# 68 of 204 expert tiles placed in the second half of the pass before them

## The chip, the cores and the metric

The kernel runs on one core of one Trainium2 chip. The metric is the device time of one execution in microseconds (us). The core has five engines, each with a program of its own that it runs strictly in order: PE (matrix multiply), DVE (vector), ACT (scalar functions), POOL (here it writes the descriptors of indirect transfers) and SP (here it issues plain transfers). They meet only through semaphores: an engine that waits for one holds back all that stands behind the wait in its program.

## What is computed

A graph layer over 12500 nodes of 256 numbers: an attention over edges (`gnn`), a linear attention over all nodes (`mix`), and then a mixture of experts on the sum. Only the last part is touched:

```python
x = x + gnn(xn) + mix(xn)                     # rows of 256, two norms inside
# then, with xn = layernorm(x) * gamma + beta:
logits = einsum('bsd,de->bse', xn, Wr) + br
top_vals, top_idx = top_k(logits, 2)          # 2 of 8 experts for each row
w = softmax(top_vals)
for e in range(8):
    h = gelu(xn @ W1[e] + b1[e])              # 256 -> 512
    y += (h @ W2[e] + b2[e]) * w_full[..., e]
x = x + y
```

## The kernel before

All stages before the last two stay as they are. The node rows stand in 98 tiles of 128 rows, in 14 chunks of 7 (CHUNK, CHUNKS).

**The pass** is `finish` (line 1479). It goes over the 14 chunks in a software pipeline; a step is one turn n of DVE's loop (line 1977). In step n DVE does `divide(n)` (L1831 scales the chunk, L1834 adds the residual row `xn` once it is loaded, then statistics), `gat_scale(n)`, `join(n-1)` (L1853 to L1862, with the other rows `hh` and `x_row`, then statistics), `choose(n-2)` (the two experts of every row, L1886 on), `ffn_scale(n-1)`, `take_slots(n-2)` and `tag(n-2)` (where each row goes in its expert's region, ending at L1946). ACT does the square roots, the affine parts (`scale_tiles`, L1721 and L1722; `make_rows`, L1742 and L1746) and the softmax's exponential; PE transposes the finished rows for the router (`turn_rows`, L1772 and L1777) and counts ranks (`rank`). POOL scatters the rows of a chunk into the experts' regions in DRAM, 14 indirect transfers a chunk (L1700). SP stores each joined chunk to `out` and loads the chunk two ahead: store, `xn`, `hh`, `x_row`, 0.9 MB each, in that order. Once in the pass it loads the weights of all eight experts, 8.4 MB, at L1656 and L1657, ahead of the loads of the last chunk. Two calls of `fold_bias` on PE (L1796) fold a vector into the first bias. Behind the last chunk DVE lists for each of 204 tiles its expert, its first row and how many adds must be done before its own (L1993 to L2031).

**The expert tiles** are `run_experts` (line 2040), in a block of their own that starts when all engines have left the pass. A tile is 128 rows of one expert. SP loads its rows (ring of 8), PE transposes them (`turn_rows`, L2139), multiplies by W1 (`up`, L2149) and W2 (`down`, L2158), ACT does gelu between (L2174), DVE copies the transposes (L2188), copies W1 to a fixed place (L2193), makes the weights and adds the bias (L2198 to L2215), and POOL adds the rows to `out` by an indirect transfer with addition (L2123). Every engine handles tile `it` together with earlier ones: PE does transposes of `it`, down of `it-3`, up of `it-1`; DVE the copies of `it`, the gate of `it-1`, the bias of `it-2` and the last addition of `it-3`. Rings of two buffers tie them: transposes of `it` wait for the copy of `it-2`, up of `it-1` for the copy of `it-1`. An add waits until all adds of earlier experts are done, since two of them may meet in a row.

## Time and profile before

| | us |
|---|---|
| median of 3 runs | 3553.38 (3551.12 to 3561.58) |
| the profiled execution | 3556.23 |
| its span, first to last instruction | 3554.6 |
| start of step 9, 10, 13 of the pass | 2528.72, 2560.27, 2652.57 |
| last routing work on DVE | 2728 |
| first up of an expert tile | 2771.67 |

All times of the trace count from the first instruction of the profiled execution. A timeline row gives the start, the duration, the engine, the source line, the operation with what it writes and reads, and in brackets how long the engine had been idle and what ended that. A row of stretches gives the length, then for each engine busy time and number of instructions (PE, PE's weight loads, DVE, ACT, POOL), then the granted clock of PE as a share of 2.4 GHz, the mean share of busy time of the 16 DMA engines and GB/s.

### The profile page before, as it was taken

The page shows a single profiled execution, that of the slowest core. Times are in us where ns is not written, and L with a number is a line of the kernel's source. Part 1 is how long each engine was busy: PE and PEld are TensorE (multiplying, and loading weights), DVE is VectorE, ACT ScalarE, POOL GpSimd, SP SyncE. Part 2 cuts the span into 40 slices and gives each one's busy share as a digit, 9 for nine tenths or more (in the row PEclk, how much of TensorE's full clock was granted, in tenths as well). Part 3 has the DMA queues.
Part 4 walks back from the last instruction along what each step waited for, and adds up shares of the span by engine and source line. Part 5 has one row for each costly group of instructions (what it writes and reads, how often), then busy time and mean ns, then how long its engine had stood idle before and what let it go on. Part 6 is the DMA issues. An engine that isn't in the chain of part 4 may idle for free. (4 is left out here: it accounts for less than half of the span.)

```text
span 3554.6 us, 70140 instructions
## 1 busy us (share of the span) xinstructions
PE 2799.0 (79%) x17326; PEld 2288.6 (64%) x17327; DVE 2343.5 (66%) x6416; ACT 1273.4 (36%) x4243; POOL 2154.7 (61%) x2117
## 2 busy tenths in 40 slices
PE   6758888889989978888888888433344899999997
PEld 4635666666666756666666666323334799999997
DVE  6656666666666667777777777888877455555554
ACT  5723333333333323333333333355542233333332
POOL 3167777777777776666666666246666344444443
PEclk9979999999999989999999999755555899999999
DMA  7645656666666666666666666445582344444443
GB/s 248 240 130 156 159 158 160 161 159 162 163 163 164 162 157 185 180 177 182 178 175 174 171 174 171 130 158 177 183 281 103 74 70 71 71 71 69 72 71 52
DMA packets 384652, 529.69 MB, mean 149 GB/s; under 512 B 64276, under 2 KB 323559, under 8 KB 384218
## 3 DMA queue, kind: packets, MB, share of 16 engines
q0 software_dynamic: 114496, 265.49, 31.9%
q1 hardware_dynamic: 185112, 183.84, 17.5%
q10 hardware_dynamic: 84770, 77.19, 6.8%
q8 instruction: 112, 1.84, 0.2%
q14 instruction: 162, 1.33, 0.1%
HBM read 394.80 MB, written 132.72 MB: 148 GB/s over the span
## 5 line engine op out<-in xcount | busy, mean ns | idle before, releaser
L1133 POOL DMA_INDIRECT rows<-node_rows,index x1552 | 1476.2, 951 | 566.3 <-issue 447.5
L1411 PE MATMUL ps_sum<-msg,hot 128*128 128x260 f32 x3904 | 1015.0, 405 | 18.4 <-DVE big L1230 2.6
L1411 PEld LDWEIGHTS ps_sum<-msg,hot 128*128 128x128 f32 x3904 | 727.5, 196 | 133.1 <-issue 7.8
L1213 DVE TENSOR_TENSOR msg<-rows,ps_w 128x1024 f32<-128x1024 f32 x488 | 595.9, 1221 | 38.0 <-ACT ps_w L1305 22.4
L2123 POOL DMA_INDIRECT out_dram<-big x204 | 353.1, 1731 | 437.2 <-DVE big L2215 388.0
L2174 ACT ACTIVATE x_actT<-x_ps_hT,b1T 128x128 f32<-128x128 f32 x816 | 232.8, 368 | 523.8 <-PE x_ps_hT L2149 523.8
L1189 DVE TENSOR_SCALAR hotT<-targets,pair_node_id 128x512 bf16 x488 | 187.0, 383 | 344.3 <-SPq L1095 340.5
L2149 PEld LDWEIGHTS x_ps_hT<-x_rowsT,x_w_now 128*128 128x128 f32 x3264 | 399.0, 193 | 11.5 <-DVE x_w_now L2193 1.1
L1391 PE MATMUL ps_hot<-ident_h,hotT 128*128 128x128 bf16 x1952 | 194.9, 223 | 268.2 <-DVE hotT L1189 266.0
L2149 PE MATMUL x_ps_hT<-x_rowsT,x_w_now 128*128 128x128 f32 x3264 | 400.1, 276 | 0.7 <-DVE x_w_now L2193 0.7
L1700 POOL DMA_INDIRECT expert_in<-f_rows,f_slot x196 | 259.4, 1323 | 223.7 <-ACT f_rows L1742 166.7
L2158 PE MATMUL x_ps_out<-big,x_actT 128*128 x1632 | 385.9, 379 | 0.0
L1391 PEld LDWEIGHTS ps_hot<-ident_h,hotT 128*128 128x128 bf16 x1952 | 128.9, 99 | 363.2 <-DVE hotT L1189 351.9
L1298 ACT ACTIVATE e<-e 128x16 f32<-128x16 f32 x488 | 106.3, 218 | 660.7 <-DVE e L1207 657.3
L2158 PEld LDWEIGHTS x_ps_out<-big,x_actT 128*128 128x128 f32 x1632 | 294.2, 190 | 31.7
L1293 ACT ACTIVATE hot<-ps_hot 128x512 f32<-128x512 bf16 x488 | 286.6, 587 | 41.0 <-PE ps_hot L1391 38.9
L2188 DVE COPY x_rowsT<-x_ps_t 128x256 f32<-128x256 f32 x204 | 86.6, 425 | 253.7 <-PE x_ps_t L2139 253.7
L1230 DVE TENSOR_TENSOR big<-big,ps_sum 128x260 f32 x488 | 202.4, 415 | 8.0 <-issue 4.8
L1759 PE MATMUL f_ps_rank<-f_taken,f_earlier 128*128 128x56 f32 x28 | 9.4, 440 | 250.0 <-DVE f_taken L1908 250.0
L1423 PE MATMUL ps_kv<-wq,area 128*128 128x512 f32 x392 | 193.6, 617 | 9.5 <-DVE area L1239 8.8
L1279 DVE TENSOR_TENSOR area<-ps_kv,area 128x256 f32<-128x256 f32 x98 | 41.6, 425 | 210.7 <-PE ps_kv L1468 210.7
L2215 DVE SCALAR_TENSOR_TENSOR big<-x_ps_out,x_weight,x_bias 128x256 f32<-128x256 f32 x204 | 98.7, 484 | 121.8 <-issue 113.6
(284 smaller groups left out, 4146.7 us busy)
## 6 DMA issues: line engine op xcount, KB each, us to landing
targets<-dst_row SPq DMA_DIRECT2D x391, 128.0 KB
big<-expert_in SPq DMA_DIRECT2D x204, 130.0 KB, 2.1
rows<-node_rows,index POOLq DMA_INDIRECT x1564
node_rows<-big SPq DMA_DIRECT2D x14, 924.0 KB
turned<-rT SPq DMA_DIRECT2D x14, 896.0 KB, 4.5
area<-turned ACTq DMA_DIRECT2D x98, 128.0 KB
queries<-area ACTq DMA_DIRECT2D x98, 128.0 KB
area<-queries ACTq DMA_DIRECT2D x98, 128.0 KB
```

Of the source, the lines that this page charges most:

```text
L1133: g.indirect_dma_start(rows[:, j, k, :], None, s.node_rows, bass.IndirectOffsetOnAxis(ap=index[:, b, j * G + k:j * G + k + 1], axis=0)).th ...
L1213: v.tensor_tensor(m[:, :, 0:D].rearrange("p g (h f) -> p g h f", h=GH), rows[:, bass.ds(here, 1), :, 0:D].rearrange("p j g (h f) -> p (j g ...
L1230: v.tensor_tensor(dest, dest, ps_sum[:, j % 2, 0:SUM], ALU.add).then_inc(sum_added, 1)
L1293: act.activation(hot[:, j % MSGS, :], ps_hot[:, 0:SPAN], ACT.Copy).then_inc(hot_ready, 1)
L1391: mm = pe.transpose(ps_hot[:, k * P:(k + 1) * P], hotT[:, j % 2, k * P:(k + 1) * P], ident_h[:, :])
L1411: mm = pe.matmul(ps_sum[:, j % 2, 0:SUM], hot[:, j % MSGS, k * P:(k + 1) * P], msg[:, j % MSGS, k, :], start=(k == 0), stop=(k == G - 1))
L1423: pe.matmul(ps_kv[:, :], rT[:, u, c * P:(c + 1) * P], s.wq[:, c, D:3 * D], start=(c == 0), stop=(c == C - 1))
L1700: g.indirect_dma_start(s.expert_in, bass.IndirectOffsetOnAxis(ap=slot[0:count, j, k, i:i + 1], axis=0), rows[0:count, j, i, :], None).then ...
L2123: g.indirect_dma_start(out, bass.IndirectOffsetOnAxis(ap=rows[:, j, D:D + 1].bitcast(I32), axis=0), outs[:, j, :], None, compute_op=ALU.ad ...
L2149: mm = pe.matmul(ps_hT[:, j % 2, k * P:(k + 1) * P], w1_now[:, j % 2, a:a + P], rowsT[:, j % 2, c, :], start=(c == 0), stop=(c == C - 1))
L2158: mm = pe.matmul(ps_out[:, j % 2, 0:D], actT[:, j % 2, c, :], s.w2[:, bass.ds(e, 1), c * D:(c + 1) * D].rearrange("p e n -> p (e n)"), sta ...
L2174: ins = act.activation(actT[:, j % 2, c, :], ps_hT[:, j % 2, c * P:(c + 1) * P], ACT.Gelu, bias=s.b1T[:, bass.ds(e * HC + c, 1)])
```

## The change

`finish` and `run_experts` become one function, `pass_and_experts`, in one block. When half of the chunks (SPLIT = 7) are routed, DVE lists 17 quads (`list_quads`, at the end of step 8): a quad is 4 tiles, 512 rows, of one expert that are surely there by then. These 68 tiles (FIRST) run inside the rest of the pass. Each step has ten positions p, and `positions` says which tiles stand at which: three in step 9 (p = 8, 9, 10); in steps 10 to 13 six at p = 4 (behind divide) and five at p = 8 (behind join); 8 in step 14, 6 in step 15, and 7 in step 16, which is new and holds the second listing, of the 136 tiles left (LATER). All five engines have their work at the same positions. The ring of a tile's stages is as before.

The weights of an early tile come from a ring of two homes (`w_ring`), loaded a quad ahead by SP and scaled there by DVE (two operations a quad); the later tiles still copy W1, into the same ring. The homes of the eight experts and of b2 are loaded one or two at a time as the pass frees the memory (`settle_homes`, from step 5 on), no more in one lot. `hh`, `x_row` and the PSUM tile of the row transposes have one buffer in place of two; SP loads `hh` and `x_row` of chunk n behind join(n-1), and `xn` of chunk n+1 behind those. On ACT the rows of a chunk (`make_row`) move from the end of one step to the start of the next, one at a position, with `scale_tile` among them from p = 5. The folds of the bias go from the end to steps 1 to 4, one expert at a time, with W1 loaded for them once more.

```diff
+SPLIT = 7
+QUAD = 4
+FIRST = QUAD * QUADS
+LATER = EX_TILES - FIRST
...
+def positions():
+    at = {}
+    it = 0
+    for n in range(CHUNKS + 3):
+        for p in range(1, 11):
+            if n == SPLIT + 2:
+                count = 1 if p >= 8 else 0
+            elif SPLIT + 3 <= n < CHUNKS:
+                count = 6 if p == 4 else 5 if p == 8 else 0
+            elif n == CHUNKS:
+                count = 0 if p < 4 else 2 if p == 7 else 1
+            elif n == CHUNKS + 1:
+                count = 1 if p in (2, 4, 6, 8, 9, 10) else 0
+            elif n == CHUNKS + 2:
+                count = 1 if p < 10 else FIRST
+            else:
+                count = 0
+            count = min(count, FIRST - it)
+            at[n, p] = range(it, it + count)
+            it += count
...
-        hh = sb("f_hh", [P, 2, CHUNK, D])
-        x_row = sb("f_x_row", [P, 2, CHUNK, D])
+        hh = sb("f_hh", [P, CHUNK, D])
+        x_row = sb("f_x_row", [P, CHUNK, D])
...
+        def first_tiles(steps, lag, n, p):
+            for it in TILES_AT[n, p]:
+                for k, step in enumerate(steps):
+                    if it - lag[k] >= 0:
+                        step(it - lag[k], (it - lag[k]) % EX_RING, (it - lag[k]) // EX_RING)
...
             @block.sync
+                def load_hx(c):
+                    full = min((c + 1) * CHUNK, TILES - 1) - c * CHUNK
+                    if c >= 1:
+                        sp.wait_ge(joined, c)
...
+                def ahead(it):
+                    if it % QUAD == 1 and (it + 3) // QUAD < QUADS:
+                        load_quad_w1((it + 3) // QUAD)
+                    if it % QUAD == 2 and (it + 2) // QUAD < QUADS:
+                        load_quad_w2((it + 2) // QUAD)
+                    if it + 4 < FIRST:
+                        load(it + 4, (it + 4) % EX_RING, (it + 4) // EX_RING)
...
+                        if n == SPLIT + 2 and p == 1:
+                            sp.wait_ge(quads_listed, 4)
+                            for j in range(ROW_RING):
+                                sp.wait_ge(scattered[j], scatters(j, SPLIT))
+                            load_quad_w1(0)
+                            load_quad_w2(0)
+                            for k in range(4):
+                                load(k, k, 0)
+                        for it in TILES_AT[n, p]:
+                            ahead(it)
+                        if p == 7 and n <= CHUNKS + 1:
+                            if n >= 2:
+                                settle_homes(n - 1)
+                            if n <= CHUNKS:
+                                store(n - 1)
+                            if n < CHUNKS:
+                                load_hx(n)
+                            if n + 1 < CHUNKS:
+                                load_xn(n + 1)
...
             @block.gpsimd
+                for n in range(3, CHUNKS + 3):
+                    name_rows(n - 3)
+                    for p in range(1, 11):
+                        if p <= CHUNK:
+                            scatter(n - 3, p - 1)
+                        first_tiles([add_rows], [3], n, p)
+                later_tiles(g, [add_rows], [3])
...
             @block.scalar
+                for n in range(CHUNKS + 3):
+                    for p in range(1, 11):
+                        if 2 <= n < CHUNKS + 2 and p <= CHUNK + 1:
+                            make_row(n - 2, p - 1)
+                        if n < CHUNKS:
+                            if p == 4:
+                                gat_root(n)
+                            if p >= 5:
+                                scale_tile(n, p - 5)
+                            if p == 10:
+                                scale_tile(n, CHUNK - 1)
+                        if p == 10 and 1 <= n <= CHUNKS:
+                            ffn_root(n - 1)
+                        if p == 10 and 2 <= n < CHUNKS + 2:
+                            odds_of(n - 2)
+                        first_tiles([look_up, gelu], [0, 1], n, p)
...
             @block.tensor
+                steps, lag = [look_up_later, turn_rows, down, up], [0, 0, 3, 1]
+                for n in range(1, CHUNKS + 3):
+                    for p in range(1, 11):
+                        if 2 <= n < CHUNKS + 2:
+                            if p <= CHUNK + 1:
+                                turn_row(n - 2, p - 1)
+                            if p == 10:
+                                rank(n - 2)
+                        first_tiles(steps, lag, n, p)
+                    if n <= 4:
+                        for e in range(2 * n - 2, 2 * n):
+                            fold_bias(e)
+                later_tiles(pe, steps, lag)
...
             @block.vector
+                def place_w1(n, j, turn):
+                    if early(n):
+                        if n % QUAD == 0:
+                            q = n // QUAD
+                            v.wait_ge(quad_w1_in[q % 2], 16 * (q // 2 + 1))
+                            for c in range(C):
+                                w = w_ring[:, q % 2, c * HID:(c + 1) * HID]
+                                v.tensor_scalar(w, w, gamma_col[:, c:c + 1], None, ALU.mult).then_inc(quad_scaled, 1)
+                        return
...
+                steps, lag = [look_up, copy_rowsT, place_w1, gate, add_bias, weigh, weigh_bias], [0, 0, 0, 1, 3, 1, 2]
+                def tiles_now(n, p):
+                    first_tiles(steps, lag, n, p)
...
                 def divide(c):
...
+                    v.wait_ge(xn_loaded[c % 2], 16 * (c // 2 + 1))
...
                     v.tensor_scalar(g[:, 2, :], g[:, 1, :], 1e-5, None, ALU.add).then_inc(root_in, 1)
+                    tiles_now(c, 4)
...
                 def join(c):
...
+                    v.wait_ge(hx_loaded, 32 * (c + 1))
...
                     v.tensor_scalar(f[:, 2, :], f[:, 1, :], 1.0 + 1e-5, 1e-10, ALU.mult, ALU.add).then_inc(ffn_root_in, 1)
+                    tiles_now(c + 1, 8)
...
+                    if n == SPLIT + 1:
+                        list_quads()
+                v.tensor_copy(end_row[0:1, :], running[0:1, :, 0]).then_inc(ends_ready, 1)
+                list_tiles()
+                later_tiles(v, steps, lag)
```

`list_quads` and `list_tiles` do what L1993 to L2031 did, over 20 and 136 columns; `list_tiles` has `tiles_now(16, p)` between its parts and ends with the scaling of all homes' W1. Before the later tiles SP waits for the last scatters, the end rows and the second list.

## Rows read from the trace of the kernel before

**Rows 1.** the page's slices: busy tenths of DVE, granted clock of PE.

```profile
DVE  6656666666666667777777777888877455555554
...
PEclk9979999999999989999999999755555899999999
```

**Rows 2.** stretches: busy us (instructions) by engine, granted clock, DMA share, GB/s.

```profile
2560.00:2647.00 87.00, 26.00 (x125) 24.48 (x123) 75.30 (x178) 45.91 (x92) 58.70 (x45) 0.50 0.71 237
...
2900.00:3000.00 100.00, 100.00 (x700) 94.51 (x699) 54.42 (x162) 30.77 (x108) 46.99 (x27) 1.00 0.44 72
```

**Rows 3.** timeline, pass: start, us, engine, line, operation, operands [idle before].

```profile
2528.72 2.02 DVE L1831 TENSOR_TENSOR big<-big,shift 128x1792 f32<-128x1792 f32 x1
...
2560.27 2.02 DVE L1831 TENSOR_TENSOR big<-big,shift 128x1792 f32<-128x1792 f32 x1
...
2561.55 0.59 ACT L1742 ACTIVATE f_rows<-big,f_ffn 128x256 f32<-128x256 f32 x1
...
2563.71 2.02 DVE L1834 TENSOR_TENSOR big<-big,f_xn 128x1792 f32<-128x1792 f32 x1 [1.42 <-DMA f_x_row<-in_x_dram]
...
2569.40 0.20 DVE L1846 RECIPROCAL f_gat<-f_gat 128x7 f32<-128x7 f32 x1 [0.28 <-ACT f_gat L1709]
...
2570.84 0.58 ACT L1721 ACTIVATE f_xn<-f_w_b,ones,f_a_mix 128x256 f32<-128x256 f32 x1
...
2583.20 0.21 DVE L1886 TENSOR_TENSOR f_logits<-f_ps_l,f_br_b 128x56 f32<-128x56 f32 x1
...
2590.57 0.17 DVE L1946 TENSOR_SCALAR f_rows<-f_lowest 128x7 f32<-128x7 f32 x1
```

**Rows 4.** timeline of the expert tiles: the first up, one whole tile.

```profile
2771.67 3.79 PE L2149 MATMUL x_ps_hT<-x_rowsT,x_w_now 128*128 128x128 f32 x16 [0.69 <-DVE x_w_now L2193]
...
3103.07 0.38 PE L2139 MATMUL x_ps_t<-ident,big 128*128 128x128 f32 x2
...
3103.28 1.89 PE L2158 MATMUL x_ps_out<-big,x_actT 128*128 x8
...
3103.83 0.68 DVE L2193 COPY x_w_now<-big 128x1024 f32 x1
...
3105.01 1.95 PE L2149 MATMUL x_ps_hT<-x_rowsT,x_w_now 128*128 128x128 f32 x16
...
3106.80 0.38 PE L2139 MATMUL x_ps_t<-ident,big 128*128 128x128 f32 x2
```

**Rows 5.** stretches, PE alone: busy us (instructions), granted clock, DMA share, GB/s.

```profile
364.00:368.00 4.00, 3.93 (x14) 0.57 0.47 120
...
2770.00:2778.00 8.00, 7.31 (x35) 0.52 0.37 89
...
228.00:232.00 4.00, 1.51 (x7) 1.00 0.70 170
```

**Rows 6.** timeline around scatters, folds and the listing of the tiles.

```profile
2552.84 0.16 POOL L1690 IOTA f_rows<- 128x7 int32 x1
...
2691.07 2.02 DVE L1853 TENSOR_TENSOR f_xn<-f_hh,f_xn 128x1792 f32<-128x1792 f32 x1
...
2696.91 13.79 PE L1796 MATMUL f_ps_fold<-f_beta_col,big 128*128 128x1 f32 x64
...
2727.89 0.27 DVE L1993 CAST f_end_row<-f_running 1x8 int32<-1x8 f32 x1
...
2746.80 0.30 DVE L2031 TENSOR_SCALAR adds_before<-f_first_tile 1x204 int32<-1x204 f32 x1
...
2751.18 0.97 POOL L1700 DMA_INDIRECT expert_in<-f_rows,f_slot  x1 [0.30 <-issue]
```

**Rows 7.** a stretch full of transfers, a quiet one, step 13's wait.

```profile
2579.80:2595.00 15.20, 8.23 (x39) 7.61 (x40) 10.89 (x45) 7.42 (x16) 6.21 (x7) 0.50 0.92 286
...
2563.70:2579.80 16.10, 2.56 (x13) 2.46 (x13) 15.51 (x22) 9.17 (x18) 13.36 (x10) 0.50 0.23 83
...
2664.21 2.02 DVE L1834 TENSOR_TENSOR big<-big,f_xn 128x1792 f32<-128x1792 f32 x1 [9.62 <-DMA f_x_row<-in_x_dram]
```

More of the change, by code:

```diff
@@ L1658, in _ @@
[L1658 removed]
+                for n in range(1, CHUNKS + 3):
[19 more added lines that the diff above has]
+                                load_xn(n + 1)
+                        if p == 10 and n <= 3:
+                            for e in range(2 * n, 2 * n + 2):
+                                load_fold(e)
+                    if n == CHUNKS + 1:
+                        sp.dma_start(out[(TILES - 1) * P:N, :], s.sums[0:TAIL, TILES - 1, 0:D]).then_inc(stored, 16)
@@ new lines, in up @@
+                def up(n, j, turn):
+                    if early(n):
+                        u = n // QUAD % 2
+                        pe.wait_ge(quad_scaled, 2 * (n // QUAD + 1))
+                    else:
+                        u = j % 2
+                        pe.wait_ge(w1_ready, n - (FIRST - 1))
+                    pe.wait_ge(x_rowsT_ready, n + 1)
+                    from_item(pe, act_ready, n, 2, n - 1)
+                    for k in range(HC):
+                        for c in range(C):
+                            a = c * HID + k * P
+                            mm = pe.matmul(ps_hT[:, j % 2, k * P:(k + 1) * P], w_ring[:, u, a:a + P], x_rowsT[:, j % 2, c, :],
+                                           start=(c == 0), stop=(c == C - 1))
+                    mm.then_inc(hT_psum, 1)
@@ new lines, in down @@
+                def down(n, j, turn):
+                    if early(n):
+                        q = n // QUAD
+                        if n % QUAD == 0:
+                            pe.wait_ge(quad_w2_in[q % 2], 16 * (q // 2 + 1))
+                    else:
+                        if isinstance(n, int) and n == FIRST:
+                            pe.wait_ge(experts_in, EXPERT_LOADS)
+                        e = expert(n, j)
+                    pe.wait_ge(act_ready, n + 1)
+                    from_item(pe, out_ready, n, 2, n - 1)
+                    for c in range(HC):
+                        if early(n):
+                            w = w_ring[:, q % 2, C * HID + c * D:C * HID + (c + 1) * D]
+                        else:
+                            w = w2[:, bass.ds(e, 1), c * D:(c + 1) * D].rearrange("p e n -> p (e n)")
+                        mm = pe.matmul(ps_out[:, j % 2, 0:D], actT[:, j % 2, c, :], w, start=(c == 0), stop=(c == HC - 1))
+                    mm.then_inc(out_psum, 1)
@@ L1811, in settle, with now @@
                     v.wait_ge(chain, done[0])
+                def now(ins):
+                    then(ins)
+                    settle()
                 def over_experts(a):
```

752 lines of the change are left out of this document (413 added, 339 removed).

## The prediction

> **What bounds the kernel now.** I read the page's 40 slices first [rows 1]. Counted from 0, slices 26 to 30 are the pass, with DVE at seven or eight tenths and PEclk at 5; slices 32 to 39 are the expert tiles, with DVE at five and PEclk at 9. The table by stretches says it in microseconds [rows 2]: in the pass DVE is busy 75.3 of 87 us and PE 26.0 at a granted clock of 0.50 (1.2 GHz); in the tiles PE is busy 100.00 of 100.00 at 1.00 (2.4 GHz), DVE 54.42, ACT 30.77, POOL 46.99. So the pass is bound by DVE, the tiles by PE, and work moved from the second under the first is worth something only as far as PE can do it while DVE does something else.
>
> **Prices of before.** One step of the pass, on DVE, step n = 10 [rows 3]: divide from 2560.27 to gat_scale at 2569.40, of which 1.42 us is a wait for a transfer and 0.28 one for ACT: A = 7.4 us. gat_scale and join with its measuring, to choose at 2583.20: B = 13.8. choose, ffn_scale, take_slots, tag, to 2590.74: C = 7.5. Steps 10 to 13 together last from 2560.27 to 2691.07 (the join of step 14 [rows 6]), 130.8 us.
> One expert tile, on PE [rows 4]: transposes 3103.07, down 3103.28, up 3105.01, next transposes 3106.80: 0.21 + 1.73 + 1.79 = 3.73 us. That is 26.8 tiles in the 100 us of [rows 2]: DVE 2.0 a tile, ACT 1.15, POOL 1.75 (and 0.3 of issue). An early tile has, in place of the 0.68 copy of W1 [rows 4], a scaling of it once in four tiles (bounded by two such copies, 0.3 a tile): I take 2 on DVE as the upper bound, 1.6 is the lower. The tail is that chain: the first up starts at 2771.67, the span ends at 3554.6, so 782.9 us for 204 tiles; after the up of tile 68 come 782.9 - 68 x 3.73 = 529, less 1 for the cold first tiles: 528.
>
> **Part 1, the tail: 68 tiles off it**, 68 x 3.73 = 253.8 us. What they cost elsewhere decides.
>
> **Part 2, before the tiles.** In step 8 list_quads is new on DVE. The listing of before takes 2727.9 to 2747.1 for 204 columns [rows 6]; at 20 columns the same pattern with operations of about 0.2 us (as choose's [rows 3]) is some 11 us. Step 9 starts that much later, so its wait for the transfer is gone. In step 9 SP first waits for the scatters of seven chunks (the one of chunk 6 is done at 2552.84 in before [rows 6] and lands 3 us later, some 16 us into the later step), then queues 1.5 MB of weights and rows ahead of the pass's own 3.7 MB and 1 MB of home weights; three tiles (first touches only, 3.5 us of DVE, PE's first up at half clock before ACT's ffn_root, some 4) make step 9 about 37 us against 31.6, and the residual for step 10 lands 3 us late. The folds (13.79 us of PE [rows 6], twice) move to steps 1 to 4, where PE has two thirds free: nothing. The weights' 8 MB, which made DVE wait 9.62 us in step 13 [rows 7], are spread over eight steps, ahead of the chunk's loads. The single buffers for hh, x_row and the row transposes: nothing, since those loads land some 11 us after one join and the next begins 21 us after it; if that cover went, join would wait, at most those 11 us a step. Loading only xn first: -2 at the start.
>
> **Part 3, steps 10 to 13, the heart.** Eleven tiles a step on DVE would be 22 us if their inputs were ready. They aren't: DVE's tile it copies transposes(it) and adds down(it-3), both of this place, and PE may not run more than two tiles ahead (transposes(it) waits for copy(it-2), up(it-1) for copy(it-1)). So after two tiles DVE goes at PE's 3.73, and all that stands behind the burst on DVE (join, choose) waits. Nor do PE's own rows start early: before the first burst it waits for ACT's four make_rows, before the second for four more, which ACT does only after the burst's last gelu. The clock: PE went through the whole pass at 0.50 [rows 2], rows of 8 to 128 columns being all it did; after idle stretches it fell and dense matmuls brought it back, at 2770 to 2778 with a mean of 0.52 over 8 us, at 364 to 368 with 0.57 over 4 us [rows 5]. A burst thus loses (1 - clock) x dense time, between 1.7 and 3.9 us; I take 2.5, nearer the shorter stretches, of which there are more. Counted from DVE's step start:
> - ACT's first rows start at -3.5 and take about 1.5 each; PE enters the burst at 3. The sixth down ends at 3 + 0.21 + 1.73 + 5 x 3.73 + 2.5 = 26.1, DVE leaves at 26.9 (it entered at 7.4).
> - B brings DVE to 40.8. PE's last up ends at 27.9, gelu 29.2; four rows and four pairs of scale_tile on ACT (a row of 0.59, a copy and two of 0.58 [rows 3], 1.85 each as they overlap) let PE in at 36.6. The fifth down ends at 36.6 + 1.94 + 4 x 3.73 + 2.5 = 56.0, DVE leaves at 56.8.
> - C: choose runs until 60.3, but ffn_scale waits for ACT: last up 57.8, gelu 1.3, three scale pairs 3.0, a table load and a root 1.5, so 63.6; then 3.4. Step: 67 us.
> A step without tiles and without the transfer's wait is 28.8: 38 us are paid for eleven tiles that cost 41 at the tail. That is nearly nothing gained.
> Transfers: a chunk's store and three loads keep the 16 DMA engines at 0.92 for 15.2 us [rows 7]; behind them on SP's queue go, at the second place, the row load of the burst's fifth tile and, in steps 10 and 11, a quad's W1. With 1 MB of home weights in steps 10, 11 and 13 and the adds' share, they land some 19 to 23 us after the join (at 37.3), 2 to 8 us after DVE wants them. I take 7.7, 2.5, 0.5 and 2 for the four steps: 281 us with the 68 for 67 and the 3 late in step 10. Bounds: 0 (all in time) and 12 a step (twice the 15.2).
>
> **Part 4, steps 14 to 16.** Steps 14 and 15 lasted 36.8 together (2691.07 to 2727.89 [rows 6]). Now each tile stands between single rows, and PE, ACT and DVE take turns: a row 1.0 on PE, the tile 3.73, its gelu and the next row on ACT 2.6: 7.3 a place in four places, 4 in the rest, with 3.8 of lead and two cold starts some 55 us for step 14; 38 for step 15. Bounds 45 and 33 (PE alone: 8 x 3.73 + 8 x 1.5 + 2.5), and 62 and 44. In step 16 the listing (17 us at 136 columns) and seven tiles (1.9 on DVE, 3.73 on PE) interleave; POOL is late next with 14 x 1.27 + 7 x 2.05 = 32 us [rows 6], its last scatter lands at 34, then the load of tile 68, 2.1, and a half-clock round of tile 65, 67: up(68) at about 46. In before the same stretch, 2727.9 to 2771.7, was 43.8 with no tile in it [rows 4, 6]. That, and not the middle, is the gain.
>
> **Sum**, from step 9 of before (2528.72 [rows 3]): after = 11 - 2 + 37 + 281 + 55 + 38 + 46 + 528 = 994; before 3554.6 - 2528.7 = 1025.9. Change -32 us: the profiled execution's 3556.23 becomes 3524, and since it lies inside the shown runs (median 3553.38, 3 us lower) I give 3522.
>
> The Trainium skill, TensorE: Matmul & The Clock Gate, HAM oscillation — how this bites in real kernels, says that matmuls cut into pieces with waits between start every piece on the slow clock. That speaks against this change, whose tiles now run at 1.00 without a break; the trace of before agrees as far as 0.50 in the pass goes. With that rule the sum is as above, without it it is rival 1.
>
> **Rivals.**
> 1. The clock holds between bursts. Then 2.5 us eight times and some 6 in the last steps are not paid: 3496. For it: at 228 to 232 PE worked 1.51 of 4 us and stayed at 1.00 [rows 5]; against: 0.50 under denser rows in the pass.
> 2. The tiles run truly beside the pass, PE far enough ahead that DVE pays only its 2 us: 11 x 2 + 28.8 = 51 a step, 16 x 4 off: 3458. Against it stand the two waits named above. This is also the case in which the change does what it says.
> 3. Slower: SP's queue. If a chunk's transfers together with the tiles' loads, adds and weights hold the last row load until 30 us after the join, each second burst ends 12 us later: +48, 3570. It decides from about 10 us a step on. For it: the engines at 0.92 already, and the 9.62 us when 8 MB stood ahead of the loads [rows 7]; against: 0.23 in the stretch between [rows 7].
> The Trainium skill, DMA: Bandwidth & Descriptors, Queues, rings and completion order, has descriptors of one ring consumed in order, which is what lets SP's tile loads stand behind the chunk's; the 9.62 us agree.
> 4. The clock doesn't rise in bursts at all: 6 x 7.5 and 5 x 7.5 make the step 103 us, +144, with the last steps about 3710. The rows at 2778 speak against it.
>
> **How the numbers follow.** Forecast 0.62 (3500 to 3545), rival 1 0.13, rival 2 0.04, rival 3 0.14, rival 4 and other chains of waits 0.07. About 0.3%, 10.7 us, is what a measurement can tell: faster below 3542.7, slower above 3564. Nearly all of the forecast and rivals 1 and 2 are faster: 0.73; its upper edge and a mild rival 3 are the same: 0.13; slower 0.14. The range leaves out rivals 2 and 4 and the far side of 3: 3488 to 3566.
>
> **What would show it.** A step of 67 to 75 us between divides in steps 10 to 13; in it DVE waiting on x_ps_t and x_ps_out for 15 us and on ffn_root for 3; PEclk 0.5 at each burst's start and 1.0 later; waits for W1 in steps 10 and 11 alone; up(68) some 46 us after the last tag. It is wrong if the four steps take under 60 or over 80 us each, or if steps 1 to 8 grow.

## The result and the profile after

The changed kernel takes 3525.29 us (median of 7 runs, 3509.66 to 3536.77), the kernel before 3561.58 (7 runs, 3551.12 to 3565.12): a ratio of 0.9906, interval 0.9882 to 0.9930. The profiled execution is 3525.29 with a span of 3523.5. The forecast was 3522, a change of -32 us; by the medians the change is -36, by the two spans shown -31.

The page's slices after, 40 of them, busy tenths of PE and DVE and granted clock, to be held against [rows 1]:

```profile
PE   6758878888889978888888888744277877999998
...
DVE  6655666656666667776777777788866665555554
...
PEclk9979999999999989999999999855577888999999
```

Counted from 0, slices 26 to 28 are the pass's first half, at a clock of 5 as in [rows 1]. Its second half, slices 29 to 33, has PE at 7 and 8 and a clock of 7 and 8, and DVE at 6 and 5 there. The table by stretches (busy us and instructions by engine, granted clock, DMA share, GB/s) cuts it at the ends of the steps, 9 to 15 in seven rows, then the stretch to the first up of the tail:

```profile
core 0: us, PE busy (x) PEld busy (x) DVE busy (x) ACT busy (x) POOL busy (x), PEclk, DMA share, GB/s
2541.30:2577.80 36.50, 13.33 (x64) 12.39 (x64) 29.40 (x77) 16.57 (x33) 7.61 (x6) 0.55 0.72 230
2577.80:2652.64 74.84, 58.00 (x334) 52.77 (x334) 44.08 (x128) 32.97 (x87) 36.63 (x26) 0.80 0.62 165
2652.64:2719.85 67.21, 55.39 (x332) 51.01 (x332) 44.01 (x129) 30.86 (x81) 36.84 (x26) 0.83 0.71 191
2719.85:2786.63 66.78, 54.17 (x332) 49.91 (x332) 43.29 (x128) 30.81 (x81) 36.71 (x26) 0.86 0.63 167
2786.63:2852.10 65.47, 54.40 (x332) 50.38 (x332) 43.90 (x129) 30.95 (x81) 36.72 (x26) 0.84 0.68 179
2852.10:2906.60 54.50, 42.41 (x252) 38.90 (x252) 31.70 (x94) 18.86 (x50) 30.48 (x23) 0.85 0.52 133
2906.60:2951.80 45.20, 36.97 (x214) 33.38 (x214) 15.36 (x66) 14.96 (x40) 23.75 (x21) 0.85 0.43 108
2951.80:2997.70 45.90, 32.15 (x209) 29.81 (x208) 32.59 (x110) 9.80 (x35) 28.34 (x21) 0.85 0.56 136
```

In steps 10 to 13 no engine is full: DVE is busy some 44 of 65 to 75 us, PE 54 to 58. Before, DVE was busy 75.3 of 87 us of the pass [rows 2]. The 22 to 31 us a step in which DVE now does nothing are the case's question. The timeline of step 10 (start, duration, engine, line, operation, and the idle time before it with what ended it) shows them:

```profile
2597.59 1.14 ACT L1983 ACTIVATE wq<-x_ps_hT,x_b1T 128x128 f32<-128x128 f32 x4 [2.59 <-PE x_ps_hT L2063]
2597.71 0.42 DVE L2144 COPY wq<-x_ps_t 128x256 f32<-128x256 f32 x1 [1.12 <-PE x_ps_t L2048]
...
2599.51 0.48 DVE L2186 SCALAR_TENSOR_TENSOR big<-x_ps_out,x_weight,scores 128x256 f32<-128x256 f32 x1 [1.19 <-PE x_ps_out L2083]
...
2601.44 0.42 DVE L2144 COPY wq<-x_ps_t 128x256 f32<-128x256 f32 x1 [1.12 <-PE x_ps_t L2048]
...
2637.84 0.88 DVE L2153 TENSOR_SCALAR x_w_ring<-x_w_ring,f_gamma_col 128x512 f32<-128x512 f32 x2 [6.56 <-DMA x_w_ring<-in_L_ffn_W_dram]
...
2649.59 0.20 DVE L2253 RECIPROCAL f_ffn<-f_ffn 128x7 f32<-128x7 f32 x1 [3.92 <-ACT f_ffn L1958]
```

Within a burst DVE waits twice a tile, 1.12 us for the transposes and 1.19 for the down, and the copies follow each other at 3.73 us, PE's pace in the tail [rows 4]. In the second burst a quad's W1 is 6.56 us late (in the same time PE waits 3.91 for a tile's rows), and at the step's end ffn's root 3.92. The cold starts stand in the next step, whose two bursts are cut here at the change of the clock:

```profile
2656.50:2659.90 3.40, 3.40 (x11) 2.83 (x12) 3.26 (x13) 0.00 (x0) 2.79 (x3) 0.52 0.22 80
2659.90:2679.50 19.60, 19.60 (x139) 18.54 (x138) 9.16 (x34) 7.21 (x22) 12.15 (x10) 1.00 0.63 135
2679.50:2688.40 8.90, 5.32 (x34) 5.03 (x32) 8.80 (x9) 7.57 (x19) 7.17 (x4) 0.73 0.71 186
2688.40:2693.40 5.00, 5.00 (x17) 4.28 (x18) 4.76 (x14) 0.03 (x1) 4.08 (x4) 0.50 1.02 346
2693.40:2709.50 16.10, 15.23 (x104) 14.21 (x104) 7.23 (x26) 4.58 (x16) 4.80 (x4) 0.98 1.06 322
```

The first burst begins with 3.4 us at 0.52 and goes on at 1.00; behind it, with only rows to turn, the clock falls, and the second begins with 5 us at 0.50.

### The profile page after: what moved, and what is told of

Same layout as the page of the kernel before. It is cut to its first block and busy times, and to the rows that moved or that the text cites. A ratio compares the mean times of both kernels' runs of the same rounds, so it can differ in the third digit from the quotient of the medians.

```text
span 3523.5 us, 69459 instructions
## 1 busy us (share of the span) xinstructions
PE 2835.9 (80%) x17326; PEld 2314.5 (66%) x17327; DVE 2318.7 (66%) x6449; ACT 1286.2 (37%) x4257; POOL 2145.2 (61%) x2115
## 5 line engine op out<-in xcount | busy, mean ns | idle before, releaser
L1420 PE MATMUL ps_sum<-msg,hot 128*128 128x260 f32 x3904 | 1027.9, 409 | 19.4 <-DVE big L1239 4.1
L1983 ACT ACTIVATE wq<-x_ps_hT,x_b1T 128x128 f32<-128x128 f32 x816 | 233.5, 369 | 563.8 <-PE x_ps_hT L2063 563.7
L2063 PEld LDWEIGHTS x_ps_hT<-wq,x_w_ring 128*128 128x128 f32 x3264 | 405.8, 195 | 17.5 <-DVE x_w_ring L2153 5.6
L2063 PE MATMUL x_ps_hT<-wq,x_w_ring 128*128 128x128 f32 x3264 | 405.2, 278 | 5.2 <-DVE x_w_ring L2153 5.2
L1912 POOL DMA_INDIRECT expert_in<-f_rows,f_slot x196 | 248.7, 1269 | 237.4 <-DVE f_rows L2320 140.4
L2083 PE MATMUL x_ps_out<-big,wq 128*128 x1088 | 257.2, 379 | 0.0
L2144 DVE COPY wq<-x_ps_t 128x256 f32<-128x256 f32 x204 | 86.5, 424 | 227.6 <-PE x_ps_t L2048 225.6
L2083 PEld LDWEIGHTS x_ps_out<-big,wq 128*128 128x128 f32 x1088 | 196.1, 190 | 21.1
L2186 DVE SCALAR_TENSOR_TENSOR big<-x_ps_out,x_weight,scores 128x256 f32<-128x256 f32 x204 | 98.5, 483 | 138.2 <-issue 129.2
L2025 PE MATMUL f_ps_t<-ident,f_rows 128*128 128x128 f32 x196 | 62.3, 419 | 145.2 <-ACT f_rowsT L1977 103.3
```

Source lines behind the costliest of these rows:

```text
L1420: mm = pe.matmul(ps_sum[:, j % 2, 0:SUM], hot[:, j % MSGS, k * P:(k + 1) * P], msg[:, j % MSGS, k, :], start=(k == 0), stop=(k == G - 1))
L1912: g.indirect_dma_start(s.expert_in, bass.IndirectOffsetOnAxis(ap=slot[0:count, j, k, i:i + 1], axis=0), rows[0:count, j, i, :], None).then ...
L1983: ins = act.activation(actT[:, j % 2, c, :], ps_hT[:, j % 2, c * P:(c + 1) * P], ACT.Gelu, bias=b1T[:, bass.ds(e * HC + c, 1)])
L2063: mm = pe.matmul(ps_hT[:, j % 2, k * P:(k + 1) * P], w_ring[:, u, a:a + P], x_rowsT[:, j % 2, c, :], start=(c == 0), stop=(c == C - 1))
L2083: mm = pe.matmul(ps_out[:, j % 2, 0:D], actT[:, j % 2, c, :], w, start=(c == 0), stop=(c == HC - 1))
```

## The experiments

Times are medians beside runs of the kernel before on the same chip (3559 to 3562 us). This table of my own gives the length of each step between the last tags of two steps (step 9 from the end of the new listing), in us. In the kernel before, steps 10 to 15 were 30.4, 31.2, 30.7, 38.5, 23.4 and 13.5. The changed kernel's own interval is 8.5 us to either side, so a difference of less than that from it is not told by the medians; and the steps are those of one profiled execution, which lay within 7.3 us of its kernel's median, only with the transfers behind place 8 13 us above it.

```
kernel                    9     10    11    12    13   10-13   14    15   median  ratio (interval)
changed kernel           36.8  74.9  67.2  66.8  65.5  274.3  54.4  45.2  3525.3  0.9906 (0.9882-0.9930)
tiles in last steps only 29.1  32.1  30.4  31.2  30.6  124.4  45.3  43.9  3538.5  0.9944 (0.9930-0.9958)
tiles in the middle only 36.6  79.0  69.0  66.9  66.5  281.5  21.0  14.3  3551.0  0.9976 (0.9966-0.9986)
clock kept               36.9  75.5  67.9  65.2  65.0  273.5  52.0  43.9  3521.9  0.9902 (0.9887-0.9916)
transfers behind place 8 36.9  68.1  74.9  75.8  68.0  286.7  54.4  45.2  3532.6  0.9925 (0.9911-0.9940)
one tile a place         36.8  72.0  71.7  71.7  71.7  287.1  52.5  45.3  3538.1  0.9935 (0.9919-0.9952)
... and rows a place late 37.3 48.9  63.1  59.1  58.3  229.5  43.8  37.1  3461.3  0.9717 (0.9701-0.9733)
root ahead of gelus      37.1  73.0  63.1  63.2  61.0  260.3  49.9  46.9  3512.0  0.9862 (0.9845-0.9878)
bursts, rows late        37.1  73.3  67.9  68.9  64.9  274.9  41.4  38.6  3504.2  0.9838 (0.9821-0.9854)
one a place, xn first    36.9  47.4  64.0  60.7  58.9  231.0  42.1  35.4  3456.2  0.9696 (0.9679-0.9712)
one a place, loads apart 37.0  48.9  50.8  52.0  53.4  205.1  42.2  35.6  3439.4  0.9655 (0.9638-0.9671)
bursts, loads apart      36.7  68.3  66.8  65.6  65.7  266.4  54.5  46.6  3512.1  0.9868 (0.9853-0.9883)
... and clock kept       36.8  67.5  61.5  60.9  61.0  250.8  51.8  44.0  3493.9  0.9820 (0.9806-0.9833)
```

**Where the gain sits: two halves of the change alone.** First no tiles in steps 9 to 13:

```diff
-QUADS = -(-(SPLIT * CHUNK * P * 2 - EXPERTS * (QROWS - 1)) // QROWS)
+QUADS = 5
...
-                count = 1 if p >= 8 else 0
+                count = 0
-                count = 6 if p == 4 else 5 if p == 8 else 0
+                count = 0
```

> Only the last steps have tiles: 20 early tiles instead of 68, eight in step 14, six in step 15, six in step 16, none in steps 9 to 13. Theory (in steps 9 to 13 DVE stands behind PE's pace, so the 47 tiles there are paid with almost what they are worth): steps 9 to 13 fall from 310.8 us to some 30 + 4 x 28.8 = 145, which is -166; 48 more tiles in the tail at 3.73 are +179; the longer listing +1: 3539 us. Rival (the tiles of the middle run beside the pass and carry the gain): as slow as before, 3560. Rival (the middle loses, the last steps carry more than the whole gain): 3525 or less.

3538.5 us, 13.2 above the changed kernel. Steps 9 to 13 fall by 157.5 us, not 166, since a step without tiles is 31 us rather than 28.8 (DVE waits 8.9 us in the four steps for the residual). So the middle is worth some 13 us, for 47 tiles that take 175 in the tail; the two intervals just touch. Second, the middle alone:

```diff
-QUADS = -(-(SPLIT * CHUNK * P * 2 - EXPERTS * (QROWS - 1)) // QROWS)
+QUADS = 12
...
-                count = 6 if p == 4 else 5 if p == 8 else 0
+                count = 6 if p == 4 else (6 if n == SPLIT + 3 else 5) if p == 8 else 0
-                count = 0 if p < 4 else 2 if p == 7 else 1
+                count = 0
-                count = 1 if p in (2, 4, 6, 8, 9, 10) else 0
+                count = 0
```

> The opposite: 48 early tiles, three in step 9, twelve in step 10, eleven in each of steps 11 to 13, none in steps 14 to 16. Theory: steps 14 and 15 fall from 99.7 us to the 36.8 of before, the stretch from the listing to the first tile of the tail from 45.9 to about 44, in all -65; 20 more tiles in the tail at 3.73 are +74.6, the twelfth tile of step 10 +3.7: 3538 us. Rival (what is gained is gained in the last steps alone, the middle gives nothing and the new listing costs 11): 3555 to 3570. Rival (the middle carries the gain, the turn-taking of steps 14 and 15 loses): 3525 or less.

3551.0 us, 13 over the theory, and the reason is a slip of mine: the tail runs in rounds of eight tiles, so with 48 early tiles it is rounded up to 160, not 156. The listing's last operation says it:

```profile
2909.70 0.23 DVE L2396 TENSOR_SCALAR x_adds_before<-f_first_tile 1x160 int32<-1x160 f32 x1
```

Four more tiles at 3.73 are 14.9; without them it would be 3536 by this estimate, which no run shows, 11 above the changed kernel. The last steps are thus worth some 11 us and the middle some 13: they share the gain, and neither carries it alone.

**The clock.** TensorE's idle time in steps 10 to 13 is filled with matmuls into a free half of a PSUM bank:

```diff
+                last_tile = [0]
+
+                def fill(count):
+                    for k in range(count):
+                        pe.matmul(x_ps_t[:, (last_tile[0] + 1) % 2, 256:512], s.ident[:, :], lnbeta_b[:, :], start=True, stop=True)
...
+                                if SPLIT + 3 <= n < CHUNKS:
+                                    fill(8)
                                 rank(n - 2)
+                                if SPLIT + 3 <= n < CHUNKS - 1:
+                                    fill(8)
+                        if SPLIT + 3 <= n < CHUNKS and p in (1, 2, 3, 5, 6, 7):
+                            fill(1 if p < 4 else 2)
                         first_tiles(steps, lag, n, p)
+                        if TILES_AT[n, p]:
+                            last_tile[0] = TILES_AT[n, p][-1]
+                        if SPLIT + 3 <= n < CHUNKS and p == 4:
+                            fill(5)
```

> Idle time of TensorE in steps 10 to 13 is filled with matmuls whose result nobody reads (128x256, 16 a step around the ranking, one to five behind each row). Theory (a burst starts at 0.5 of the clock and pays for it): the stretch of 3.4 us at 0.53 at the start of each of the eight bursts goes, 1.6 to 2.0 us each, and the steps fall from 65 to 75 us by 3 to 4 each: 3525 - 14 = 3511 us, less up to 4 us that the filling itself delays. Rival (DVE, not PE's clock, sets the burst's length): no change, 3525, or longer by the filling. Rival (the rows come late by the filling): the second burst starts later and the steps grow by 2 to 4 each, 3533 to 3540.

The clock is held through the first burst of step 11 and into the second, as two stretches of that run show:

```profile
2652.00:2657.00 5.00, 5.00 (x34) 4.67 (x34) 4.83 (x17) 0.67 (x3) 3.82 (x4) 1.00 0.43 103
...
2685.00:2689.00 4.00, 3.45 (x24) 2.90 (x23) 3.79 (x17) 1.14 (x4) 1.88 (x2) 1.00 1.01 275
```

Yet the four steps are as long as before, 273.5 against 274.3. The waits over those steps (engine, line, what it waited for: us in all, times, longest) say where it went:

```profile
PE x_ps_t L2048 <- DMA big<-expert_in: 14.2, 4, 6.0
...
DVE x_w_ring L2169 <- DMA x_w_ring<-in_L_ffn_W_dram: 8.9, 2, 8.7
```

PE, sooner at the second burst, waits there for its rows 14.2 us in four times, where the changed kernel's waits for rows are 5.9 in three. The clock's price can't be read from this run: the transfers are late next.

**The transfers behind the second burst's loads.**

```diff
-                        if p == 7 and n <= CHUNKS + 1:
+                        if p == (8 if SPLIT + 3 <= n < CHUNKS else 7) and n <= CHUNKS + 1:
```

> In steps 10 to 13 SP queues the chunk's store, the home weights and the chunk's three loads behind the loads of the second place's five tiles, not ahead of them. Theory (the transfers ahead are what the second burst waits for): the wait for W1 in step 10, 6.6 us, and that in step 11 with the late row, about 3 us, go; step 10 falls from 74.9 to about 68, step 11 from 67.2 to 65, the rest stays, the residual lands some 10 us later and still ahead of its add: 3525 - 9 = 3516 us. Rival (SP's order doesn't matter, the weights are late by themselves): 3525. Rival (the chunk's loads are now late for join or for the residual's add, each step waits 5 to 10 us more): 3545 to 3565.

Step 10 falls to 68.1 and its wait for W1 is gone, as expected, but steps 11 and 12 rise to 75 and 76: the residual is late, up to 11 us.

```profile
DVE big L2200 <- DMA f_xn<-residual: 24.7, 3, 11.0
```

The theory's 3516 is missed. The mechanism is that of the rival that called this order harmful, but its 3545 to 3565 didn't come either: 3532.6 is 7 above the changed kernel, and the intervals overlap, so no loss can be told by the time. Putting the block elsewhere on SP's queue moves the wait.

**Bursts or single tiles.** One tile to a place, two in the fourth:

```diff
-                count = 6 if p == 4 else 5 if p == 8 else 0
+                count = 2 if p == 4 else 1
```

> The eleven tiles of a step in 10 to 13 stand one to a place (two in the fourth), between DVE's own operations, in place of bursts of six and five. Theory (a tile between single rows makes PE, ACT and DVE take turns: a row waits for ACT, which stands behind the gelu of the tile before, which waits for PE): 7.3 to 10 us a place in the eight places that have a row, 4 in the rest: 75 to 85 us a step, 3550 to 3590 us. Rival (the bursts themselves are what DVE pays for, and between its own operations a tile costs DVE its 2 us): 28.8 + 22 = 51 to 56 us a step, 3465 to 3475. Rival (PE's work sets the step whatever the order): 3525.

3538.1 us and 71.7 a step, a little better than the theory's 3550 to 3590 and 75 to 85. The four steps are 12.8 us longer than with the bursts; the times' intervals overlap a little. The timeline of step 11 shows the turns: ACT waits for PE's up, PE then for ACT's copy of a row, and the tile's transposes follow each other at 6.73 us.

```profile
2665.53 1.14 ACT L1983 ACTIVATE wq<-x_ps_hT,x_b1T 128x128 f32<-128x128 f32 x4 [6.48 <-PE x_ps_hT L2063]
...
2667.58 0.41 PE L2025 MATMUL f_ps_t<-ident,f_rows 128*128 128x128 f32 x2 [2.18 <-ACT f_rowsT L1977]
...
2668.19 0.41 PE L2048 MATMUL x_ps_t<-ident,big 128*128 128x128 f32 x2
...
2674.92 0.42 PE L2048 MATMUL x_ps_t<-ident,big 128*128 128x128 f32 x2
```

The same with PE's rows one place behind ACT's, from step 10 on:

```diff
-                            if p <= CHUNK + 1:
+                            if n < SPLIT + 3 and p <= CHUNK + 1:
                                 turn_row(n - 2, p - 1)
+                            if n >= SPLIT + 3 and 2 <= p <= CHUNK + 2:
+                                turn_row(n - 2, p - 2)
```

> As the run before, one tile to a place, and from step 10 on PE turns a row one place after ACT has made it (place p turns row p-2, not p-1), so that PE never waits for ACT's row of the same place. Theory (DVE stands behind PE's pace in a burst, and the turn-taking is what forbids the other order): without the turn-taking a step is DVE's own 28.8 and 11 x 2, or PE's 11 x 3.73 and eight rows at 0.9, whichever is longer, 50 to 51, with gaps 54 to 58 in place of 68.6; 4 x 12 = -48, and steps 14 and 15 some 15 less: 3455 to 3480 us. Rival (each place still waits for all three engines): 70 to 85 a step, 3530 to 3590. Rival (the transfers behind place 7 hold the tiles of the places after it as they hold the second burst): 62 to 66 a step, 3490 to 3510.

3461.3 us, inside the theory's range, though by another sum than its 54 to 58 a step. Step 10 is 48.9, and the engine that fills it is PE, busy 47.2 us of it: 11 times 3.73 and eight rows of 0.9 are 48.2. DVE is busy 42.9.

```profile
2576.95:2625.86 48.91, 47.18 (x329) 44.40 (x330) 42.91 (x129) 31.61 (x81) 38.06 (x26) 0.97 0.62 155
```

In a step without tiles, as the kernel with tiles in the last steps only shows, it is busy 26.4 of 30.4:

```profile
2602.46:2632.89 30.43, 10.21 (x48) 9.54 (x47) 26.40 (x67) 15.84 (x33) 20.11 (x15) 0.50 0.65 207
```

So a tile in pieces costs DVE 1.5 us. Steps 11 to 13 are 58 to 63. There the third rival's mechanism holds as well, though not its 3490 to 3510: in steps 10 to 13 the transfers are late.

```profile
PE x_ps_t L2048 <- DMA big<-expert_in: 31.2, 3, 12.5
...
DVE big L2202 <- DMA f_xn<-residual: 17.3, 2, 10.8
```

**ACT's order.**

```diff
+                            if p == 8 and SPLIT + 3 <= n < CHUNKS:
+                                for i in range(3, CHUNK):
+                                    scale_tile(n, i)
+                                ffn_root(n - 1)
-                            if p >= 5:
+                            elif p >= 5 and not (p > 8 and SPLIT + 3 <= n < CHUNKS):
                                 scale_tile(n, p - 5)
-                            if p == 10:
+                            if p == 10 and not SPLIT + 3 <= n < CHUNKS:
                                 scale_tile(n, CHUNK - 1)
-                        if p == 10 and 1 <= n <= CHUNKS:
+                        if p == 10 and 1 <= n <= CHUNKS and not SPLIT + 3 <= n < CHUNKS:
                             ffn_root(n - 1)
```

> In steps 10 to 13 ACT scales the last three tiles of the next chunk and takes ffn's root in place 8, ahead of the gelus of the second burst, not in place 10 behind them. Theory (ACT's order costs DVE the wait on ffn_root, 12.8 us in four steps): those waits go, the odds come in time, 3 us a step: 3525 - 12 = 3513 us. Rival (the scaling ahead of the burst holds ACT's rows and with them PE's entry): the second burst 3 to 4 us later, 3525 to 3530.

3512.0 us. The four steps are 14.0 shorter; the wait for ffn's root, 12.8 us in the changed kernel, is gone from the list of waits. In the changed kernel it is:

```profile
DVE f_ffn L2253 <- ACT f_ffn L1958: 12.8, 4, 3.9
```

**Rows one place late, bursts kept** (the second diff of the single tiles alone):

> Bursts as they are, and from step 10 on PE turns a row one place after ACT has made it. Theory (steps 14 and 15 are bound by PE and ACT taking turns, 7.3 and some 10 us a place): a place falls to about 5 us, steps 14 and 15 together from 99.7 to 80 to 85; in steps 10 to 13 PE enters each burst one row sooner, 1 to 2 us each, of which the transfers take back the second one's: 3525 - 15 - 6 = 3504 us. Rival (those steps are bound by the row loads or the clock, not by turns): 3520 to 3525.

3504.2 us, as expected in all, but all of it is steps 14 and 15: together 80.0 in place of 99.6. In steps 10 to 13 the 6 us that I gave to PE's earlier entry are not there (274.9): PE comes sooner and waits 14.4 us for its rows, DVE 9.4 for W1, as with the clock kept.

```profile
PE x_ps_t L2048 <- DMA big<-expert_in: 14.4, 4, 6.3
DVE x_w_ring L2155 <- DMA x_w_ring<-in_L_ffn_W_dram: 9.4, 2, 9.0
```

**The transfers, with single tiles.** First only their order at place 7 of steps 10 to 13, residual ahead:

```diff
+                        if p == 7 and SPLIT + 3 <= n < CHUNKS:
+                            if n + 1 < CHUNKS:
+                                load_xn(n + 1)
+                            load_hx(n)
+                            settle_homes(n - 1)
+                            store(n - 1)
+                        elif p == 7 and n <= CHUNKS + 1:
...
```

> One tile to a place and rows one place later, as two runs before (3461 us), and in steps 10 to 13 SP issues the chunk's transfers in the order in which they are wanted: residual, hh and x_row, home weights, store (it was home weights, store, hh, x_row, residual). Theory (in steps 11 and 12 of that run the step is bound by what stands ahead on SP's queue: the residual 10.8 and 6.5 us late, the row load of a tile 12.5 and 9.6): the waits for the residual, 17.3 us, go, the row loads stay behind the same bytes and hold the tile of place 2 to 4 instead, so that about half of it is gained: 3450 us. Rival (the sum of the bytes binds, whatever the order): 3461. Rival (the residual alone was late): 3444.

The residual's waits go, but PE now waits 34.5 us for tile rows, and the four steps are 231.0 against 229.5. The times' intervals overlap: no gain that can be told. Then the block taken apart, and the home weights of three steps moved behind step 13:

```diff
+                        if SPLIT + 3 <= n < CHUNKS:
+                            if p == 7 and n + 1 < CHUNKS:
+                                load_xn(n + 1)
+                            if p == 9:
+                                load_hx(n)
+                        if SPLIT + 4 <= n <= CHUNKS and p == 2:
+                            store(n - 2)
...
+                            if n == CHUNKS:
+                                settle_homes(SPLIT + 2)
+                                settle_homes(SPLIT + 3)
+                            elif n == CHUNKS + 1:
+                                for freed in range(SPLIT + 4, CHUNKS + 1):
+                                    settle_homes(freed)
```

> As that, but in steps 10 to 13 the transfers are taken apart: the residual in place 7, hh and x_row in place 9, the store in place 2 of the next step, and the home weights of steps 10, 11 and 13 in the two steps behind 13, so that no row load stands behind more than 1.9 MB. Theory (the step is bound by single loads behind a block on the queue): steps 11, 12 and 13 fall from 63, 59 and about 53 us to the 49 of step 10, -28, of which the weights take back 4 to 8 in steps 14 and 15: 3438 us. Rival (the sum of the bytes binds): 3455 to 3461. Rival (the weights or the store are now late for the tail or for the rows of the next chunk): 3465 or more.

3439.4 us, the best of all, 122 below the kernel before. Every step is now 49 to 53; PE is busy 46 to 48 of it and DVE 43, and in the middle of step 11 PE and DVE are both without a gap (last row, 14 us):

```profile
2575.00:2623.90 48.90, 47.18 (x329) 44.38 (x330) 42.97 (x129) 31.64 (x81) 38.02 (x26) 0.97 0.64 155
2623.90:2674.60 50.70, 46.54 (x333) 43.63 (x332) 42.91 (x128) 31.57 (x81) 35.65 (x23) 1.00 0.78 212
...
2726.70:2780.10 53.40, 45.62 (x313) 42.23 (x311) 43.12 (x129) 31.76 (x82) 43.52 (x28) 0.94 0.85 215
...
2643.00:2657.00 14.00, 14.00 (x106) 13.32 (x105) 14.00 (x22) 9.01 (x26) 12.37 (x6) 1.00 0.67 160
```

Whether it is the smaller blocks or the 3 MB fewer in these steps was not told apart.

**The clock again, with the transfers out of the way.** The last two kernels are the bursts of the changed kernel with the transfers taken apart as above, without and with the fillings:

> The bursts of six and five as in the changed kernel, with only the transfers of steps 10 to 13 taken apart: the residual in place 7, hh and x_row in place 9, the store in place 2 of the next step, the home weights of steps 10, 11 and 13 in the two steps behind 13. Theory (the block of transfers holds the second burst of steps 10 and 11 and hardly that of 12 and 13): the waits for W1 of 6.6 and 0.9 us and the late row of 2.2 go, 3525 - 10 = 3515 us. Rival (the transfers also cost the bursts by being at work beside them): 3500 to 3508.

> As the run beside it, and TensorE's idle time in steps 10 to 13 filled with matmuls that nobody reads, as in the run with the clock kept. Theory (the clock's cold start costs each of the eight bursts some 2 us, and in the run with the clock kept the transfers took it back in the second bursts): 8 x 2 = 16 us less than the run beside it, 3499 us. Rival (the fillings delay the rows by as much as the clock gives): 3512 to 3516, as without them. Rival (the clock's price is larger, 2.5 to 3.5 a burst): 3487 to 3495.

3512.1 us, 13 below the changed kernel and near the theory's 3515: the waits for W1 and rows, some 10, are gone and the four steps 7.9 shorter. With the fillings 3493.9, another 18.2 less, inside the last rival's 3487 to 3495 where the theory said 3499; the four steps are 15.6 shorter and steps 14 and 15 5.3. Step 12 without them, and with them:

```profile
2703.60:2769.20 65.60, 54.37 (x332) 50.35 (x332) 43.75 (x127) 30.80 (x80) 36.65 (x26) 0.84 0.69 182
```

```profile
2700.10:2761.00 60.90, 60.01 (x393) 54.35 (x393) 42.96 (x127) 30.82 (x80) 36.79 (x26) 1.00 0.74 192
```

The clock goes from 0.84 to 1.00 and the step from 65.6 to 61. In steps 11 to 13 that is 14.7 us for six bursts, 2.5 each; in step 10 0.9 in all. The fillings begin only in step 10, and its first burst starts at 0.50 in both kernels (over the first 7.6 us of the step without them and 7.9 with them).

## Why the prediction came out, point by point

**The sum.** From 2528.72 the prediction adds up to 994 us; the trace has 994.8 up to its end. Its terms, predicted and measured: the new listing less the start's 2 us, 9 and 12.5; step 9, 37 and 36.5; steps 10 to 13, 281 and 274.3; step 14, 55 and 54.5; step 15, 38 and 45.2; step 16 to up(68), 46 and 45.9; the rest, 528 and 525.8. Two terms missed by 7 and cancel: that the sum comes within a microsecond is luck, since single terms miss by up to 7.

**Part 3, the heart: right.** That DVE goes at PE's pace in a burst and what stands behind the burst pays for it is shown three ways: by the waits of 1.12 and 1.19 us a tile, by the middle being worth 13 us of its 175, and by the single tiles with late rows, where the same eleven tiles cost DVE 1.5 us each, under the 1.6 that was the lower bound, and a step 48.9. The signs named came in the main: steps of 65.5 to 74.9, some 18 us a step of DVE's idle time ahead of the copies of x_ps_t and the additions of x_ps_out (15 forecast), waits for W1 in steps 10 and 11 alone, up(68) 46 us after the last tag. The case in which the tiles run truly beside the pass (rival 2) was therefore wrong for this kernel; its 51 us a step and 3458 came nearly true for another order of the same work, but there PE, and not DVE, fills the step. The two waits named against it were real, but they are long only in bursts.

**The clock: right in size, but terms were added that don't add.** 2.5 us a burst was taken; 2.5 is measured in steps 11 to 13, and half a microsecond a burst in step 10. But clock, PE's entry and transfers were added as separate terms, and in the second bursts of steps 10 and 11 they are alternatives: whoever comes first waits for the other. Rival 1 would have given 26 us by the sum, and the fillings alone gave 3, within what can be told from none; only with the transfers apart is it 18.

**Transfers: over-charged.** 12.7 us were taken for the four steps; the 281 is 4 times 67 and these 12.7, and the 3 for the late residual in step 10 that stand beside them are not to be found in it. What the waits show is 6.6 in step 10, in step 11 1.0 for W1 and 0.9 for a row, and in step 12 1.1 for a row, 9.6 in all; the kernel with the transfers apart is 7.9 shorter in these steps. That is 3 to 5 of the 6.7 by which the four steps came out shorter; steps 12 and 13 are 66.8 and 65.5 where the sum had 67.5 and 69. For the rest no cause is shown. Rival 3, the queue binding from 10 us a step on, did not come true here, but it did in the single-tile kernel, where the steps are short enough for it.

**Step 15: wrong, and outside its bounds** (33 to 44, measured 45.2). The term took one row of 1.0 and one tile of 3.73 a place. In step 15 tiles stand in every second place, so that two rows and two of ACT's rows lie between tiles, and the clock fell on the way (0.85 in the step, 0.66 from 2925 to 2935), which a bound by PE's full pace leaves out. The timeline after:

```profile
2914.71 1.15 ACT L1983 ACTIVATE wq<-x_ps_hT,x_b1T 128x128 f32<-128x128 f32 x4 [6.50 <-PE x_ps_hT L2063]
...
2916.76 0.41 PE L2025 MATMUL f_ps_t<-ident,f_rows 128*128 128x128 f32 x2 [2.19 <-ACT f_rowsT L1977]
...
2918.80 0.43 DVE L2144 COPY wq<-x_ps_t 128x256 f32<-128x256 f32 x1 [5.11 <-PE x_ps_t L2048]
...
2928.99 3.62 PE L2083 MATMUL x_ps_out<-x_w_ring,wq 128*128 128x256 f32 x8
```

The copies of two tiles are some 10 us apart (2918.80 and 2929.23), and a down takes 3.62 us where one in the tail takes 1.89 [rows 4]. With PE's rows a place later the step is 38.6, 6.6 less, at a clock of 0.91; how much of that is the turns and how much the clock was not separated.

**"That, and not the middle, is the gain": wrong.** By the sum steps 14 to 16 with their 21 tiles gain 20 us, and the middle with the listing 11 (47 tiles, 175.3, for 164.6 more up to the end of step 13). Against the kernel before the trace gives 13 and 14; against the changed kernel the two half kernels, which keep a listing, say 11 and 13. The miss of step 15 is the difference in the last steps.

**Small ones.** The listing took 12.3 us, not 11. The start's 2 us were 0.9 at the end of step 7 and gone at the end of step 8 (the last tag at 2528.78 against 2528.65 before). Step 9, steps 14 and 16 and the tail are within 2.2. ffn's root was late by 12.8 us in four steps, the 3 each that were forecast, and the kernel with ACT's order changed gives them back.

The Trainium skill, TensorE: Matmul & The Clock Gate, HAM oscillation — how this bites in real kernels, says that matmuls cut into pieces, with waits between that are long enough, start each piece slow. The bursts agree, 0.52 over 3.4 us and 0.50 over 5. The single tiles of steps 10 to 13 are cut finer, but with shorter waits between, and they kept the clock: 0.94 to 1.00 in the best kernel.

## What to carry to other kernels

Work given to an idle engine costs the others what they wait for inside it, so place it in pieces between their own operations rather than in bursts, and look for the pair of engines that then take turns. Pieces alone were no gain here (3538 against 3525); one place of lag between producer and consumer took 21 us off with the bursts and 77 with single tiles. Terms that end at the same wait are not added but compared, and taking one away shows the next, so price them by a kernel in which the other is gone. Watch a queue's blocks when steps get shorter: what was hidden in 67 us was the bound in 50.

## What the runs showed of the hardware

Short waits cost little of the clock in these steps: with single tiles and turns, PE was busy 52.05 of 72.00 us in step 10 and had to wait about 2.2 us ahead of each row, and the granted clock was 0.92.

```profile
2576.50:2648.50 72.00, 52.05 (x332) 47.60 (x332) 43.48 (x128) 31.81 (x81) 35.79 (x26) 0.92 0.56 151
```

With the bursts PE was busy 58.00 of 74.84 us in that step, at a clock of 0.80; part of that busy time is the slow clock's own.

POOL's issue of an indirect transfer, mostly 0.97 us, was up to five times as long beside large operations of DVE. In the kernel with single tiles and the transfers apart, one that begins with the first of two operations of a whole chunk takes 4.79:

```profile
2755.09 2.02 DVE L2245 TENSOR_TENSOR f_hh<-f_xn,f_x_row 128x1792 f32<-128x1792 f32 x1
...
2755.10 4.79 POOL L1925 DMA_INDIRECT expert_in<-f_rows,f_slot  x1 [0.30 <-DVE big L2201]
```

In the kernel with the middle alone one starts 0.47 us into DVE's scaling of the home weights, two operations of 4.62 us together, and ends with them:

```profile
2909.27 0.97 POOL L1912 DMA_INDIRECT expert_in<-f_rows,f_slot  x1 [0.31 <-issue]
...
2910.08 4.62 DVE L2403 TENSOR_SCALAR big<-big,f_gamma_col 128x4096 f32<-128x4096 f32 x2
2910.55 4.27 POOL L1912 DMA_INDIRECT expert_in<-f_rows,f_slot  x1 [0.30 <-issue]
2915.12 0.97 POOL L1912 DMA_INDIRECT expert_in<-f_rows,f_slot  x1 [0.30 <-issue]
```

The Trainium skill, SBUF — State Buffer, Who interferes with whom, says that DVE's tensor_scalar can take a pair of ports that it shares with GpSimd, and that the one which comes second is blocked for the whole operation; the rows of the tensor_scalar agree in their length, but POOL's issue outlasts the first of the two operations as well. No run tried it by itself.
